# A graph network's aggregation layers: a slot's eight row gathers issued in four pairs, the later pairs behind TensorE's steps

## The reference

```
e = edge_attr @ We.T + be
m = concatenate([x[dst], x[src], e], axis=-1) @ Wp.T + bp
cnt, ssum = segment_sum(ones, dst, n), segment_sum(m, dst, n)
mean, std = ssum / cnt, sqrt(max(segment_sum(m * m, dst, n) / cnt - mean * mean, 0) + 1e-5)
mn, mx = segment_min(m, dst, n), segment_max(m, dst, n)
agg = concatenate([mean, mn, mx, std, ssum])
out = concatenate([x, agg, agg * amp, agg * att]) @ Wo.T + bo
x = relu(batch_norm(out @ Wl.T + bl))
```

## Time and profile before

| | us |
|---|---|
| median of 3 runs | 12742.13 |
| lowest, highest | 12732.27, 12769.19 |
| span of the profiled execution | 13058.8 |
| first aggregation layer, from its first scan to its last, 208 groups | 6063 to 9463 |
| second aggregation layer | 9582 to 12984 |

### The profile page before, as it was taken

How to read it: one execution, slowest core, us unless ns; L and a number is a source line. 1 busy time by engine, 2 the same in 40 slices (tenths; PEclk the granted TensorE clock), 3 DMA queues, 4 the chain that set the end, 5 groups by cost and what they waited for, 6 DMA issues and landing times. The chain is left out here.

```text
span 13058.8 us, 166557 instructions
## 1 busy us (share of the span) xinstructions
PE 8138.5 (62%) x53406; PEld 6241.7 (48%) x53407; DVE 4466.3 (34%) x5989; ACT 2268.9 (17%) x3783; POOL 5588.0 (43%) x5903
## 2 busy tenths in 40 slices
PE   5676667666666666665565665565655555555565
PEld 3444444455555555554444444444444444444444
DVE  5444444211112111113333333333443333333334
ACT  4444444100000000001111111111111111111112
POOL 3333332444443444443444444444344444444443
PEclk8877888777776776776777777777777777777777
DMA  4333334344445444443111111111111111111111
GB/s 144 143 136 142 138 139 142 133 164 164 164 164 168 165 164 164 164 164 89 42 42 42 45 41 45 42 38 42 42 57 41 42 42 42 44 41 39 42 43 53
DMA packets 409727, 1226.47 MB, mean 94 GB/s; under 512 B 119675, under 2 KB 212947, under 8 KB 360990
## 3 DMA queue, kind: packets, MB, share of 16 engines
q1 hardware_dynamic: 207943, 741.50, 15.8%
q0 software_dynamic: 188528, 235.73, 7.8%
q10 hardware_dynamic: 13160, 248.08, 4.8%
HBM read 943.27 MB, written 281.57 MB: 94 GB/s over the span
## 5 line engine op out<-in xcount | busy, mean ns | idle before, releaser
L2095 POOL DMA_INDIRECT data<-q_rows,idx x3328 | 3159.9, 949 | 3809.6 <-ACT idx L2223 2722.0
L971 POOL DMA_INDIRECT data<-h_parts,idx x2508 | 2382.6, 950 | 3422.0 <-PE p_part L986 2505.3
L1101 PE MATMUL p_z<-hs,adj 128*128 128x192 bf16 x22442 | 2779.3, 276 | 1291.2 <-issue 1277.0
L1101 PEld LDWEIGHTS p_z<-hs,adj 128*128 128x128 bf16 x22442 | 2189.8, 109 | 1981.3 <-issue 1799.9
L2299 DVE TENSOR_TENSOR_SCAN run<-reset,run,p_turn 128x1024 f32<-128x1024 bf16 x416 | 976.3, 2347 | 2841.3 <-DMA nodes<-kept_quads 2407.5
L2126 PE MATMUL part<-hot,back 128*128 128x128 f32 x6688 | 1069.2, 315 | 738.0 <-ACT back L2228 387.1
L2115 PE MATMUL p_back<-ident,run 128*128 128x128 f32 x3344 | 596.9, 338 | 1250.3 <-DVE run L2299 1206.8
L2126 PEld LDWEIGHTS part<-hot,back 128*128 128x128 f32 x6688 | 973.9, 226 | 736.6 <-issue 736.0
L2228 ACT COPY back<-p_back 128x1024 f32<-128x1024 f32 x418 | 423.2, 1012 | 5115.9 <-PE p_back L2115 3092.3
L2115 PEld LDWEIGHTS p_back<-ident,run 128*128 128x128 f32 x3344 | 509.5, 179 | 1632.7 <-issue 1632.6
L2121 PE MATMUL part<-hot,t 128*128 128x128 f32 x6688 | 1036.4, 321 | 254.8 <-issue 254.4
(11 more groups left out here) (363 smaller groups left out, 6537.6 us busy)
## 6 DMA issues: line engine op xcount, KB each, us to landing
adj<-counted SPq DMA_DIRECT2D x304, 1568.0 KB
counted<-adj ACTq DMA_DIRECT2D x76, 3136.0 KB
reset<-flags SPq DMA_DIRECT2D x208, 512.0 KB
data<-q_rows,idx POOLq DMA_INDIRECT x3328
data<-h_parts,idx POOLq DMA_INDIRECT x2508
feat<-in_ea_blocks SPq DMA_DIRECT2D x208, 128.0 KB
ea<-in_ea_cols SPq DMA_DIRECT2D x154, 88.0 KB, 1.9
rden<-node_rows SPq DMA_DIRECT2D x50, 256.0 KB
```

The costliest lines, as they stand in the source:

```text
L971: pool.indirect_dma_start(out=data[:, p % HELD, j, 0:PARTS], out_offset=None, in_=table[:, :], in_offset=bass.IndirectOffsetOnAxis(ap=idx[ ...
L1101: mm = pe.matmul(p_z[:, 0:PARTS], adj[:, (q + LAG) % 2, hi, :], hs[:, hi, :], start=(hi == 0), stop=(hi == BLOCKS - 1))
L2095: pool.indirect_dma_start(out=data[:, r, j, :], out_offset=None, in_=q_rows[:, :], in_offset=bass.IndirectOffsetOnAxis(ap=idx[:, r, j:j + ...
```

## The change

Only POOL's program in `pna_pass` changes. Ahead of the third, fifth and seventh gather of a group stand new waits, for s_back, s_turn and s_part at k * 4 + r - 4, each with a gate. The first two turns are written out, and their first five groups have no new waits; the loop begins at turn 2.

```diff
@@ -2086,16 +2086,27 @@
 
         @block.gpsimd
         def _(pool):
-            with pool.Fori(0, TURNS) as k:
+            steps = {2: s_back, 4: s_turn, 6: s_part}
+
+            def gather(k, r, paced):
+                pool.wait_ge(s_idx[r], k + 1)
+                pool.wait_ge(s_t, k * SLOTS + (r + 1))
+                gate(pool)
+                for j in range(G):
+                    if paced and j in steps:
+                        pool.wait_ge(steps[j], k * SLOTS + (r - SLOTS))
+                        gate(pool)
+                    pool.indirect_dma_start(
+                        out=data[:, r, j, :], out_offset=None, in_=q_rows[:, :],
+                        in_offset=bass.IndirectOffsetOnAxis(ap=idx[:, r, j:j + 1], axis=0),
+                    ).then_inc(s_row[r], 16)
+
+            for k in (0, 1):
                 for r in range(SLOTS):
-                    pool.wait_ge(s_idx[r], k + 1)
-                    pool.wait_ge(s_t, k * SLOTS + (r + 1))
-                    gate(pool)
-                    for j in range(G):
-                        pool.indirect_dma_start(
-                            out=data[:, r, j, :], out_offset=None, in_=q_rows[:, :],
-                            in_offset=bass.IndirectOffsetOnAxis(ap=idx[:, r, j:j + 1], axis=0),
-                        ).then_inc(s_row[r], 16)
+                    gather(k, r, k == 1 and r > 0)
+            with pool.Fori(2, TURNS) as k:
+                for r in range(SLOTS):
+                    gather(k, r, True)
 
         @block.tensor
         def _(pe):
```

## The result

The kernel after takes **12089.72 us** (median of 3 runs, 12078.66 to 12093.02) against 12742.13: ratio 0.9483 [0.9461, 0.9505], 652 us less. The forecast was 12210 (529 less), with 11970 to 12400 as its own range.

What follows compares the result with a forecast made beforehand. Bound: unbroken runs of POOL's gathers in the aggregation layers hold back TensorE's signals. 490 + 52 = 542 us of the profile, scaled by 0.976 to 529, gave 12210 us; own range 11970 to 12400, 8 in 10 11900 to 12750.

Steps and rivals of the forecast that it cites:

- Pair 1: New wait ahead of a group's third gather, for s_back of group g-5: can never hold, 0 us.
- pairs 2 and 3: Waits ahead of fifth (s_turn) and seventh gather (s_part): hold in 57 and 57 groups, and 17 and 18 more.
- The pause of pair 2: POOL's stop ahead of the fifth gather: TensorE's news comes 2.6 us later, held gathers start 3.1 us later than before.
- a held pair 2: POOL stopped ahead of the fifth gather in 114 groups: next burst 4.3 us earlier on average, 490 us in all.
- Pair 3: Wait ahead of the seventh gather, held by s_part alone: 35 times 1.5 us, 52 us.
- The sum: Both aggregation layers: 490 + 52 = 542 us of the profiled execution, 13058.8 to 12517 us.
- The scaling: Profiled gain times 0.976, since the profile is 317 us above the runs' median: 529 us, so 12213, said as 12210.
- make_t's DMA wait: make_t, reader of the gathered rows in aggregation: its wait for a DMA stays near 34 us.
- A: Resumed four gathers block TensorE's next signal nearly each time: gain only 205 us, 12540 us; chance 0.18.
- C: Gather bursts aren't the cause; held gathers delay p_back's signal: 240 us slower, 12980, or 12860; chance 0.08.
- D: Delayed gathers reach their users after all, giving back 462 of the 542 us: 12660 us; chance 0.02.
- B: TensorE's lateness is made by recording the profile; outside it the pause meets nothing: no change, 12742 us; chance 0.10.

Runs made afterwards that it cites:

- s_back alone: Kernel after with only the new wait for s_back, ahead of the third gather, kept: 13078.59 us, ratio 1.0005 to the kernel before.
- the second profile: Profile of the kernel after, run again unchanged in a later set: 12405.54 us, ratio 0.9475 to the kernel before beside it.
- s_turn alone: Kernel after with only the new wait for s_turn, ahead of the fifth gather, kept: 12487.04 us, ratio 0.9555 to the kernel before.
- the repeated before: The kernel before, built and run once more unchanged for a second trace: 13092.7 us against 13072.17, ratio 1.0004.
- the alike pair: Later profiles of the unchanged kernels before and after, from sets where the kernel before took 13072 and 13094 us; spans differ by 670 us.
- the kernel with 72 fills: Kernel after, its new waits replaced by 72 one-column fills of a spare buffer on POOL ahead of the fifth gather: 11448.79 us, ratio 0.8947.
- the one with 12: Kernel after, its new waits replaced by twelve five-column fills of a spare buffer on POOL ahead of the fifth gather: 13125.08 us, ratio 1.0027.
- the convolutions with two breaks: Kernel after, new waits replaced by waits for own landed gathers: first four in aggregation, first four and eight of eleven in convolutions; 10622.1 us, 0.8312.
- s_turn at the start: Kernel after with, as its only new wait, the one for s_turn moved ahead of a group's first gather: 12087.14 us, ratio 0.9238.
- the own landing: Kernel after, its new waits replaced by one ahead of the fifth gather for the group's own first four to land: 11462.85 us, ratio 0.8963.

## Why the prediction was right, and where its terms were off

**Pair 1 (0 us).** Right: s_back alone measured 1.0005, with no hold.

**How often pairs 2 and 3 hold.** Predicted 57 and 57 for s_turn, 17 and 18 more for s_part. Measured 57 and 60, 24 and 22; in the second profile 57 and 56, 26 and 28. Replaying the old trace against the new questions gave the counts almost exactly for s_turn. s_part's are higher; that the group behind a held one comes earlier than the replay could know would give this, but no run tests it.

**The pause of pair 2.** Taken as 2.6 us of drain and a restart at 3.1 us after the place of the thirteenth gather. In the pair shown: drain 2.3 us, the thirteenth 2.74 us later than unbroken. Right.

**What a held pair 2 gives: the mis-sized term.** I had the transposes of p_back end 3.7 us into the resumed run and then halved their fate, "late about every second time", for a mean of 4.3 us. The 3.7 us was right (3.72 in the pair shown). The lateness wasn't: of 107 such cases in the trace after, 1 was late. So nearly every held group gains the full shift. Joined pairs measure 24.5 us from start to start at the median against 30.2 before: 5.7 us. 114 x 5.7 = 650 where I had 490; s_turn alone gave 608. The error was to take the age of the run as what decides. Signals of p_back 3.69 us into a run were late in the trace of before, others at 4.89 us on time, so no finer bin of age would have helped. What parts them is how many matmuls TensorE had started since the run's first gather: of before's signals that ended less than 6 us into a run, all 262 with at most 22 were on time and all 159 with 27 or more were late (in the repeated before the same but for one at 27). In the resumed runs of the kernel after TensorE had started 9 to 12, since it had been waiting for the scan. The count is not all of it: 19 signals over 6.6 us into a run were late with 12 to 18, and in the kernels with a pause in every group it parts them less cleanly.

**Pair 3.** 52 us predicted, 663 - 608 = 55 measured, though by a different split: 46 to 54 holds at about 1.1 us each, not 35 at 1.5. That the product fits is partly luck.

**The sum.** 542 predicted for the profiled run, 663 measured between the two profiles taken alike; the 529 became 652.

**The scaling.** I took the given profile's 317 us above the median as something of that execution and scaled the gain by 0.976. In later sets the kernel before ran at 13072 and 13094 us without anything changed in it: the difference was one between sets of runs. To scale was right all the same, since 0.9483 and 0.9475 show that the share is what stays; only its reason was wrong.

**make_t's DMA wait** was to stay near 34 us: 19.1, and 31.4 in the alike pair (26.1 before). Right. The scan's idle time was to fall by about 250 us per layer and fell by 341, in the alike pair by 393 (1475.6 to 1082.5). The layers were to be near 3130 us: 3002 and 3022, in the alike pair 3085 and 3079. "Everything before 6063 us unchanged": 6070.9 and 6068.9 in the alike pair.

**The rivals.** A (the resumed gathers block the next signal): refuted by the 1 of 107, and by 608 us against its 205. C (bursts not the cause, so a hold only delays): refuted, above all by the kernel with 72 fills, which waits for no other engine and gives 10.5%, while the one with 12 gives nothing. D (late rows reach their users): refuted for this change by make_t's row. It comes true in two of the experiments: in the convolutions with two breaks, and in the kernel with 72 fills, where make_t waits for its rows 41 times, 210.4 us in two layers. The rule beside it, issue early and wait late (the Trainium skill, DMA: Bandwidth & Descriptors, Rules for kernel authors), holds for the transfer, and no run contradicts that its cost can be hidden; but it prices only the DMA, and here issuing eagerly held up another engine. B (the lateness exists only under recording) can't have its forecast right: the time did fall by the 5%. But the profiled run of the kernel after is itself one of the timed runs (12078.66 us, span 12076.9), and every timed run has a recorded span. Whether an unrecorded execution shows the lateness at all stays open; no run here could tell.

**Point by point in time.** Sum, over layer one, of the time from the modelled end of p_turn to its scan and of p_back to its copy: in the alike pair 1250 + 379 = 1629 us before and 869 + 425 = 1294 after. The difference, 335 us, is nearly the layer's 340.5. Beyond that it isn't one to one: s_turn at the start has 683 + 230, 381 us less than the kernel after beside it, for 148 us of layer. These ends are modelled, but the recorded semaphore updates say the same: in the burst of the earlier trace rows TensorE's own update for p_turn stands at 8117.59, 16 us after the transposes, while the gathers' landings are told all through the burst. The late news is TensorE's: over 5.5 us into a run, 1 of its 481 updates is recorded within 0.3 us of its instruction's end, while of those updates of VectorE and ScalarE that are recorded within 10 us (many are missing), 270 of 279 are.

**Open.** Why gathers hold TensorE up is not settled: the runs show when it happens, not by what path. That a number of TensorE's own matmuls parts late from on time is a hint, but no run tells whether the program or its recording (rival B) makes it so. And why a pause in the middle of each group (0.8963) beats a cut between groups (0.9238) is clear only in where the time lies: the usual group takes about the same, 11.98 and 12.22 us at the median in layer one, but with the cut 40 groups take over 14 us, 417 us above 12.2 in sum, and with the own landing 24, 198 us above. The 24 all stand beside a block of finished nodes, at some 20 us; with the cut the groups there take some 26 us, and 17 others 15 to 20. Why they do was not worked out.

## What to carry to other kernels

When an engine's answer comes late and no semaphore explains it, lay the late ones against the other engines' issue streams, not only against what they wait for; here a late signal was a matter of how far TensorE had worked into POOL's unbroken run of gathers. A producer that runs ahead on an idle engine isn't free: break its stream every few instructions, and measure a plain pause against a tied wait: here the plain one (the stream's own landing) gave 10.4%, the change 5.2% and the best tied wait 7.6%. Then look whether the producer has become the bound, as POOL did here. When a replay of the old trace decides a term and the cases behind it split in half, as at "every second time", look for the quantity that parts them before taking the mean.

## What the runs showed of the hardware

- Indirect gathers issued back to back by POOL (0.94 us each, 1.25 us apart) delay TensorE in the profiled runs: in the aggregation layers its signals pass while it has started at most 22 matmuls since the run's first gather and are held from 27 on (signals of the kernel before less than 6 us into a run), mostly until 1.8 to 3.1 us past the last gather; in the convolutions its p_z matmuls fall from 8 to some 2 per us. VectorE's and ScalarE's updates there are not late where recorded (270 of 279 within 0.3 us).
- 0.65 us between two gathers after each four doesn't help, 2.4 us (a landing) or 3.4 us (the fills) does: ratio 1.0027 against 0.8963 and 0.8947. Lengths between weren't run.
- POOL may compute during the silence: in the kernel with 72 fills signals come out while it fills.
- With the layers denser the granted clock rose by the way, 0.74 in the earlier trace rows, 0.77 after, 0.81 with the own landing, while PE's busy time for layer one fell only from 2004.76 to 1951.99 us.
- The same kernel's median moved from 12742 to 13094 us from one set of runs to another, 2.8%, while the kernel after's ratio stayed within 0.1% (0.9483 and 0.9475).
